# First head of a chunked delta-rule attention: diagonal blocks solved on VectorE, value convolutions summed on GpSimd, first step reordered

## What is computed

```python
mixed = silu(causal_conv(hidden @ w_qkv, conv_w))      # 4 taps along the tokens
q, k, v = split(mixed); q, k = l2norm(q) / sqrt(128), l2norm(k)
beta = sigmoid(hidden @ w_b); g = -exp(A_log) * softplus(hidden @ w_a + dt_bias)
def step(state, t):                                     # per value head, state is 128x128
    state = state * exp(g_t)
    delta = (v_t - k_t @ state) * beta_t
    state = state + outer(k_t, delta)
    return state, q_t @ state
o = rmsnorm(outs * silu(hidden @ w_z)) * norm_gamma; x = x + o @ w_out
```

## Time and profile before

| | |
|---|---|
| time, median of 3 runs | 1442.57 us (1440.33 to 1448.05) |
| the profiled execution | 1443.81 us, its span 1441.8 us |
| PE busy | 1299.2 us, 90% of the span |
| DVE (VectorE) busy | 965.2 us, 67% |
| ACT (ScalarE) busy | 836.3 us, 58% |
| POOL (GpSimd) busy | 758.8 us, 53% |

### The profile page before, as it was taken

One profiled execution on the slowest core, in us unless ns is written; L12 is line 12 of the kernel. 1 busy time (PEld: TensorE's weight loads), 2 busy tenths in 40 slices (PEclk: granted clock), 3 DMA queues, 4 the chain that ended last, 5 costly groups with the idle time before them and its releaser, 6 DMA issues. The chain is left out here.

```text
span 1441.8 us, 24494 instructions
## 1 busy us (share of the span) xinstructions
PE 1299.2 (90%) x8392; PEld 875.2 (61%) x8392; DVE 965.2 (67%) x1918; ACT 836.3 (58%) x2136; POOL 758.8 (53%) x1241
## 2 busy tenths in 40 slices
PE   6658999999999999999999999988897899899894
PEld 4345666666666667666667666666545466555673
DVE  5947678887788787887878788754602366641454
ACT  3646777787677876777768777665432455420121
POOL 1674866868668676686676866841000000117363
PEclk9969999999999999999999999989999999999897
DMA  2535265654755646547465474556101950202687
GB/s 81 152 87 114 66 163 135 172 139 112 188 131 145 158 112 174 140 132 185 105 187 135 115 190 127 134 126 181 55 0 34 375 156 1 81 17 104 133 186 188
DMA packets 234955, 188.06 MB, mean 130 GB/s; under 512 B 163858, under 2 KB 202854, under 8 KB 229968
## 3 DMA queue, kind: packets, MB, share of 16 engines
q1 hardware_dynamic: 228688, 177.97, 45.8%
q0 software_dynamic: 6144, 8.53, 3.3%
HBM read 121.16 MB, written 65.70 MB: 130 GB/s over the span
## 5 line engine op out<-in xcount | busy, mean ns | idle before, releaser
L1294 DVE SCALAR_TENSOR_TENSOR heads_y<-psum_banks,gdn_conv_w,heads_y 128x1021 f32<-128x1021 f32 (+2 forms) x192 | 244.7, 1275 | 66.4 <-ACT heads_y L1089 63.3
L789 PE MATMUL psum_banks<-main_hT,gdn_w_in 128*128 128x512 f32 x512 | 255.6, 607 | 12.7 <-DVE heads_y L1294 6.7
L1591 POOL TENSOR_TENSOR heads_XT<-heads_XT,heads_tmp 128x126 f32<-128x126 f32 (+22 forms) x496 | 198.0, 399 | 38.9
L1588 POOL TENSOR_TENSOR heads_tmp<-heads_XT,heads_A 128x126 f32<-128x126 f32 (+22 forms) x496 | 197.1, 397 | 39.8
L1122 ACT ACTIVATE heads_O<-psum_banks,heads_coef 128x128 f32<-128x128 f32 x224 | 69.5, 362 | 124.4 <-PE psum_banks L820 124.3
L1570 POOL TENSOR_TENSOR heads_v_s<-heads_v_s,heads_k_root 128x2048 f32<-128x2048 f32 x16 | 58.3, 3643 | 151.1 <-DMA heads_v_s<-values_by_tokens 151.1
L848 PE MATMUL psum_banks<-heads_w_z,main_hT 128*128 128x256 f32 x512 | 131.9, 392 | 0.0
L789 PEld LDWEIGHTS psum_banks<-main_hT,gdn_w_in 128*128 128x128 f32 x512 | 90.8, 194 | 61.7 <-issue 49.3
L854 PE MATMUL psum_banks<-heads_ogT,heads_w_o 128*128 128x512 f32 x240 | 118.6, 607 | 0.0
L1089 ACT ACTIVATE heads_y<-psum_banks,gdn_conv_w 128x1024 f32<-128x1024 f32 x64 | 71.1, 1111 | 55.5 <-PE psum_banks L789 55.5
L848 PEld LDWEIGHTS psum_banks<-heads_w_z,main_hT 128*128 128x128 f32 x512 | 94.9, 198 | 10.2
(11 more groups left out here) (287 smaller groups left out, 3010.8 us busy)
## 6 DMA issues: line engine op xcount, KB each, us to landing
heads_Dm<-cum_dram SPq DMA_DIRECT2D x16, 1024.0 KB, 4.8
values_by_tokens<-heads_v_s SPq DMA_DIRECT2D x64, 256.0 KB, 3.9
heads_v_s<-values_by_tokens SPq DMA_DIRECT2D x16, 1024.0 KB, 5.8
outputs_by_features<-heads_ogT SPq DMA_DIRECT2D x120, 128.0 KB, 2.5
heads_ogT<-outputs_by_features SPq DMA_DIRECT2D x30, 512.0 KB, 3.9
main_w_gu<-in_w_gu SPq DMA_DIRECT2D x4, 2816.0 KB, 20.9
gdn_w_in<-in_w_in SPq DMA_DIRECT2D x16, 512.0 KB, 5.3
heads_A<-kk_blocks SPq DMA_DIRECT2D x64, 128.0 KB, 5.0
```

Source lines behind the costliest of these rows:

```text
L789: ins = pe.matmul(out[:, half * 512:(half + 1) * 512], w_in[:, kd_, j * P:(j + 1) * P], hT[:, kd_, half * 512:(half + 1) * 512], start=kd_ ...
L1294: dve.scalar_tensor_tensor(y[j][:, shift:T], src[:, 0:T - shift], conv_w[:, head, j, t:t + 1], y[j][:, shift:T], ALU.mult, ALU.add).then_i ...
L1588: pool.tensor_tensor(tmp[:, 0:n, 0:m], bc_last(XT[:, 0:n, j], m), bc_mid(A0[:, j, j + 1:BLK], n), ALU.mult).then_inc(solve_step.sem, 1)
L1591: pool.tensor_tensor(XT[:, 0:n, j + 1:BLK], XT[:, 0:n, j + 1:BLK], tmp[:, 0:n, 0:m], ALU.add).then_inc(solve_step.sem, 1)
```

## The change

For head 0 alone:

1. `eliminate(0)` leaves GpSimd and becomes `eliminate_first()` on VectorE, with the same instructions in the same order. The scaling of `A0` was VectorE's already and moves into it. GpSimd's `eliminate` now serves heads 1 and later only.
2. The 6 taps of the two value convolutions of head 0 leave VectorE. ScalarE writes each tap's product (PSUM times one weight) to a borrowed room in SBUF, and GpSimd adds it to `y[j]`. There are 4 rooms, so the fifth and sixth products wait for the first and second sums.
3. The transpose `kt` of head 0 moves from step 0 into the prologue, ahead of the wait for the gate sums.
4. Step 0 has another order on TensorE (attn0 and attn1 ahead of p2), VectorE and SyncE's DMA queue (the inverse's store ahead of the values' store). ScalarE's table is unchanged.

```diff
 PE_FIRST = banked(rows("""
 1: p0/-1 p1/-1
 2: norm_q/0
+3: attn0/1 attn1/2
 4: p2/-1 p3/-1
 5: kk0/3 p4/-1 p5/-1
 6: kk1/0
 7: p6/-1 p7/-1
-8: attn0/1
-9: attn1/2
 13: y6a/3 y6b/0
...
 DVE_FIRST = rows("""
-0: kt
-2: norm_q tap00 tap01 tap02
 3: vt0
-4: vt1
-6: tap10 tap11 tap12
-7: decay0 decay1 decay2 decay3 tap20 tap21 tap22
-8: attn0
-9: attn1
-10: turn scales tap30 tap31 tap32
+4: vt1 norm_q
+5: tap00 tap01 tap02
+6: turn decay0 decay1 decay2 decay3
+7: attn0 attn1
+8: tap10 tap11 tap12
+9: tap20 tap21 tap22
+10: scales tap30 tap31 tap32
 16: inverse0
 17: inverse1
...
-SP_FIRST = """kt_out kt_in values_out values_in products_out inverse_out products_in inverse_in w_in""".split()
+SP_FIRST = """kt_out kt_in inverse_out values_out inverse_in values_in products_out products_in w_in""".split()
...
+    s_prod = a.sem("first_tap_products")
+    rooms = [ogT[:, n].rearrange("p a i j -> p (a i j)") for n in range(2)] + [og[0][:, C * n:C * (n + 1)].rearrange("p a b -> p (a b)") for n in range(2)]
+
+    def tap_product(j, t):
+        return rooms[(3 * (j - 2) + t) % 4]
...
+            def tap_products(j):
+                for t in range(3):
+                    n = 3 * (j - 2) + t
+                    if n >= 4:
+                        act.wait_ge(conv_done.sem, n + 3)
+                    act.activation(tap_product(j, t)[:, 0:T - 3 + t], first_pairs[j][:, 0:T - 3 + t], ACT.Copy,
+                                   scale=conv_w[:, 0, j, t:t + 1]).then_inc(s_prod, 1)
...
             act.activation(q(GAMC), tot, ACT.Exp).then_inc(s_a, 1)
+            tap_products(2)
             conv_base(3, 0, first_pairs[3], 4)
+            tap_products(3)
             act.wait_ge(s_v, 13)
...
+            def eliminate_first():
+                dve.wait_ge(loaded["own_row"], 16)
+                dve.wait_ge(cb_ready.sem, cb_ready.done(0, "it"))
+                dve.tensor_tensor(A0[:], A0[:], bc_mid(cb[:], BLK), ALU.mult).then_inc(solve_step.sem, 1)
+                dve.tensor_tensor(XT[:], own_row[:], bc_mid(cb[:], BLK // 2), ALU.mult).then_inc(solve_step.sem, 1)
+                for j in range(BLK - 1):
+                    n, m = j // 2 + 1, BLK - 1 - j
+                    dve.wait_ge(solve_step.sem, solve_step.ahead(0, f"m{j}"))
+                    dve.tensor_tensor(tmp[:, 0:n, 0:m], bc_last(XT[:, 0:n, j], m), bc_mid(A0[:, j, j + 1:BLK], n),
+                                      ALU.mult).then_inc(solve_step.sem, 1)
+                    dve.wait_ge(solve_step.sem, solve_step.done(0, f"m{j}"))
+                    dve.tensor_tensor(XT[:, 0:n, j + 1:BLK], XT[:, 0:n, j + 1:BLK], tmp[:, 0:n, 0:m], ALU.add).then_inc(solve_step.sem, 1)
...
             dve.tensor_copy(q4(G_), by_head(g_c)).then_inc(s_v, 1)
+            evacuate(0, "kt")
             dve.wait_ge(s_cum, 2)
...
             block_scales(0)
-            dve.wait_ge(cb_ready.sem, cb_ready.done(0, "it"))
-            dve.tensor_tensor(A0[:], A0[:], bc_mid(cb[:], BLK), ALU.mult).then_inc(solve_step.sem, 1)
             dve.wait_ge(s_a, 6)
             dve.tensor_scalar(q(NGAM), q(GAM), -1.0, None, ALU.mult).then_inc(s_v, 1)
             dve.tensor_tensor(tot, tot, diff, ALU.subtract).then_inc(s_v, 1)
-            first_convolution(2)
-            first_convolution(3)
+            eliminate_first()
             dve.wait_ge(s_limit, 1)
...
-            pool.wait_ge(loaded["own_row"], 16)
             pool.wait_ge(s_const, 1)
-            eliminate(0)
+            pool.wait_ge(conv_done.sem, 6)
+            for j in (2, 3):
+                for t in range(3):
+                    shift = 3 - t
+                    pool.wait_ge(s_prod, 3 * (j - 2) + t + 1)
+                    pool.wait_ge(conv_done.sem, 3 * j + t)
+                    pool.tensor_tensor(y[j][:, shift:T], y[j][:, shift:T], tap_product(j, t)[:, 0:T - shift], ALU.add).then_inc(conv_done.sem, 1)
```

More of the change, by code:

```diff
@@ L1572, in eliminate @@
             def eliminate(h):
-                if h:
-                    pool.wait_ge(cb_step.sem, cb_step.done(h, "rnd"))
-                    pool.tensor_tensor(cb[:], rnd[:], beta_rows[:, h], ALU.mult).then_inc(cb_ready.sem, 1)
+                pool.wait_ge(cb_step.sem, cb_step.done(h, "rnd"))
+                pool.tensor_tensor(cb[:], rnd[:], beta_rows[:, h], ALU.mult).then_inc(cb_ready.sem, 1)
                 pool.wait_ge(cb_ready.sem, cb_ready.done(h, "it"))
-                if h:
-                    pool.tensor_tensor(A0[:], A0[:], bc_mid(cb[:], BLK), ALU.mult).then_inc(solve_step.sem, 1)
-                    key_root(h)
+                pool.tensor_tensor(A0[:], A0[:], bc_mid(cb[:], BLK), ALU.mult).then_inc(solve_step.sem, 1)
+                key_root(h)
                 wait(pool, xd_stored, xd_stored.base(h), 16)
                 pool.tensor_tensor(XT[:], own_row[:], bc_mid(cb[:], BLK // 2), ALU.mult).then_inc(solve_step.sem, 1)
-                if h:
-                    b = bank_of(h - 1, "u6a")
-                    pool.wait_ge(full[b].sem, full[b].done(h - 1, "u6a"))
+                b = bank_of(h - 1, "u6a")
+                pool.wait_ge(full[b].sem, full[b].done(h - 1, "u6a"))
                 for j in range(BLK - 1):
```

## The result

The changed kernel takes 1466.18 us (median of 4 runs, 1464.4 to 1474.75) against 1441.45 us for the kernel before in the same session (4 runs, 1436.81 to 1448.05): the ratio is 1.0191, 95% interval 1.0155 to 1.0227. (The ratios here are those on record with the runs; the quotient of the two medians is 1.0172.) The forecast was 1470.0 in a range of 1450 to 1476. The profiled execution took 1464.4 us, its span 1462.3.

A forecast was written before the change was run, and what follows sets the result against it. Bound taken: from step 2 TensorE, before that a dependence chain through head 0's solve. Store 77.1 + 33.1 to y6a + 14.7 = scan start 124.9, 27.2 us later than 97.75; median 1470 us, range 1450 to 1476.

The forecast's parts named there:

- scan start: First product of the scan with the finished inverse; forecast at 124.9 us against 97.75, 27.2 us later.
- the first term of the sum: Time at which head 0's solved blocks are stored, forecast at 77.1 us.
- the other two: Intervals from the blocks' store to y6a, forecast 33.1 us, and from y6a to the scan start, 14.7 us.
- D: Rival, 5%: no change, within some 5 us, from A's E, warm TensorE, B's 5 us and shorter small instructions.
- A: Rival, 22%: VectorE and GpSimd don't hold each other up during the solve; E at 64.0, scan start 111.8, 1457 us.
- B: Rival, 10%: step 1 gives back 5 us through earlier head-1 scales; 1465 us, or 1452 with A's E.
- the last rival: TensorE's clock doesn't fall in the gaps: 3.6 us less, up to 4 more; 1462 us; within the main case's 55%.
- E: End of head 0's solve, when its blocks are stored; forecast 77.1 us, 2.7 later than before.
- E to y6a: From the blocks' store to TensorE's y6a, with head 1's first work behind the solve; forecast 33.1 us against 8.65.
- C: Rival, 8%: the solve's length alone decides, y6a waits only for the turn, 8.3 us earlier; 1434 us.
- y6a to the scan start: From TensorE's y6a to the scan's first product; forecast to stay at 14.74 us, later taps lying beside the chain.
- The moves that cost nothing: Early kt, ScalarE's products, GpSimd's sums and early attn were claimed to fit idle time before the solve's end.

The follow-up runs named there:

- e1: Changed kernel with GpSimd's six tap sums cut to 8 elements each, leaving head 0's value convolutions incomplete; ratio 1.0096 to the kernel before.
- e4: Changed kernel with two moves in VectorE's table: tap10 to tap12 ahead of the turn, head 1's scales ahead of tap20 to tap22; ratio 1.0104 to before.
- e3: Kernel before with the new order tables and kt in the prologue, solve still on GpSimd, all taps on VectorE; ratio 1.0145 to before.
- e8: Kernel before with XT and 6 of 31 pairs on VectorE, kt in the prologue, inverse's store and load ahead of the products'; ratio 1.0009.
- e7: Kernel before with XT and the first 6 of head 0's 31 solve pairs on VectorE, the other 25 on GpSimd; ratio 1.0026.
- e2: Changed kernel with the old order tables of TensorE, VectorE and SyncE in step 0, kt still in the prologue; ratio 1.0113 to before.
- e9: Kernel before with kt in the prologue and the inverse's store and load ahead of the products', whole solve on GpSimd; ratio 1.0012.
- e5: Changed kernel with the six value taps back on VectorE ahead of its solve, no ScalarE products or GpSimd sums; ratio 1.0149 to before.
- e6: Changed kernel with the table moves of e4 and the value taps back on VectorE as in e5; ratio 1.0086 to before.

## Why the prediction was right

The mechanism and the size held: 26.9 us later at the scan start, where 27.2 was forecast. That it is this close is in part luck: the first term of the sum was 2.9 us too long and the other two 1.7 and 0.9 too short, and they cancelled. D falls with A, whose short solve it needs, and with B. TensorE's clock did fall in the gaps: the projections that follow them took 5.49 and 6.46 us, so the last rival falls too.

- **The solve.** E was forecast at 77.1 and is 74.2. That VectorE gets about one instruction in for each sum was right, and e1 shows it. From the first sum to the end of the last, 16.7 us were forecast (42.4 to 59.1) and 14.6 measured (42.35 to 56.90): a sum takes 2.0 us where little of VectorE's lies in it (4.19 for the first two), not 2.3. Four of the 62 were done by then too; I had started them all after the sums. The 62 small instructions at 18.0 us were right: 17.0 for 58.
- **E to y6a.** Forecast 33.1, measured 34.8. The links were the forecast ones: tap0 done at E + 6.7 (forecast 7.1), the exponentials at 97.25, E + 23.0 (22.4), the taps of the queries at about 102.6, E + 28.3 (27.7). p6 and p7 took 6.46 us instead of 5.4 after 12.3 us of idle time. The decays took 5.94 instead of 3.2, because one mask ran against a 4.03-us product of GpSimd (below), and ended at 93.03 instead of E + 14.5. It cost nothing: ScalarE, which had waited for p4 and p5, started the exponentials at 92.47 and ran all 16 without a gap. In e4, where they began earlier, they did wait for a mask, by 0.38 us.
- **The store, load and turn.** Forecast: turn at E + 9 after a wait of 2 us, ahead of the bound. Measured E + 10.6 after a wait of 3.94 us. It doesn't set y6a: C falls. In e3 the turn's wait is 20.7 us, and there too y6a goes by p7.
- **y6a to the scan start.** Forecast 14.7, measured 15.6: the evacuation starts 3.0 us after y6a (112.01), 2.1 before, as ScalarE does base3 and the norms of head 1 first, and base3 waits for p6 and p7, which end just as y6a starts.
- **Step 1.** Forecast about 65 us, measured 65.06. B falls. Of the two items that the prediction put ahead of `scales`, base3 is the one that held it (109.21, after 11.96 us of waiting for p7); tap22 had ended at 106.4. The reciprocal at 110.60 is 14.0 us ahead of the scan start, as before.
- **The moves that cost nothing.** Right for the kernel's end, with one exception that did no harm: the keys' store, now issued beside weight loads, took 7.32 us to issue against 3.09 before, but its load still went out earlier (53.74 against 60.57).
- **From the scan start to the median.** The scan is 26.9 us later, the two profiled executions differ by 20.6 us and the medians by 24.7. The ratio with its interval puts the difference at 22 to 33 us, so the forecast of 27 at the scan start passes on to the time as far as these runs can tell. In the traces the delay stays 25.1 to 27.3 us up to the 15th state copy and is 22.5 at the 16th. There the two profiled executions differ in TensorE's clock: 0.77 in the kernel before (930 to 960 us) and 0.94 in the changed one (956 to 986). That points to the executions and not to the change, but no run separates them; the runs of one kernel spread by 10 us.

## What to carry to other kernels

A chain of short dependent instructions on VectorE should not run beside long GpSimd instructions on SBUF: each link can wait for a whole one. When work moves onto an engine whose order is fixed, look at what that order puts behind it and who waits for that: here the solve was not longer, and yet the scan began 27 us later. In an order table an item that waits for a DMA goes behind the items that are already ready and that others wait for: moving the taps so, and the scales up, was worth 11.9 us here. A shorter piece is only worth what the next wait lets through: of 1.9 us won on the solve 0.8 were left in e8 and less than nothing in e7. And times counted from the start of a trace should be counted again from an item just ahead of the change: e2 and e9 began up to 3 us early, and read from zero e9 seemed to gain 1.2 us where it lost 1.5.

## What was not expected of the hardware

- VectorE waits out what is left of GpSimd's instruction, however small its own is: 0.19 us became 1.70 (32 elements) and 1.87 (31 elements). One mask of 512 elements met a product of 2048 elements (timelines of the changed kernel, VectorE and GpSimd):

```profile
88.90 4.13 DVE L1411 TENSOR_TENSOR heads_Dm<-heads_Dm,heads_limit 128x512 f32<-128x512 f32 x1
```

```profile
88.45 4.03 POOL L1595 TENSOR_TENSOR heads_v_s<-heads_v_s,heads_k_root 128x2048 f32<-128x2048 f32 x1 [9.57 <-DMA heads_v_s<-values_by_tokens]
```

- An instruction with one tensor operand can wait too, when by these rows it starts second. The scaling of 256 elements at 44.44 began 0.04 us ahead of GpSimd's second sum and took 0.24 us; the product of 256 elements right behind it took 2.21. The same scaling took 1.35 us in the kernel before, 1.36 in e3 and 1.38 in e9, where it came while GpSimd's XT was running, and 0.25 in e1, e5 and e6.
- The time to issue a DMA was longer right behind other transfers. The keys' store took 7.32 us behind the weight loads and 3.09 before, 11 us after them; the inverse's store took 1.27 us by itself, 2.10 in e2 and 2.90 in e7 right behind the kk store. That the others in flight are the cause was not tested.
- Eight projections of TensorE took 3.60 us without a gap before them (e4, granted clock 1.00 from 88 to 92 us). In the changed kernel they took 5.49 after 18.59 us of idle time and eight small products (0.66 from 83 to 90 us), and 6.46 after 12.3 us of idle time (0.57 from 102 to 109.2).
